# Hybrid block on one core: narrow products between the norm's halves, z tiles in the decay chain, the last output product in two parts, squares added on GpSimd

## The reference

```python
# part 1: 32 heads of 64, state 128 (one B, C per head)
proj = LN(x) @ Win.T                      # x_ssm, z, B, C, dt
xc, Bc, Cc = silu(causal_conv4(...))      # each
h = exp(dt*A) * h + (dt*xc) outer Bc;  y = h . Cc
y = y * rsqrt(mean(y*y) + 1e-6) * silu(z);  x += y @ Wout.T
# part 2 and 4: 16 routed experts, the best 2 by sigmoid, and 2 shared
y = gelu(x @ g) * (x @ w1 + b1) @ w2 ;  x += sum_e weight_e * y_e   (x: normalized)
# part 3: 64 heads of 8, state 128, one B, C for all
x_, B, C = silu(causal_conv4(...)); dt = softplus(.)
state as above; y = y + D*x_
y = y * rsqrt(mean(y*y over 512) + 1e-5) * norm_w * silu(z);  x += y @ out_proj
```

## Time and profile before

| what | us |
|---|---|
| median of 3 runs | 1175.32 (1175.06 to 1180.73) |
| the profiled execution | 1177.91 |
| its span, first to last instruction | 1176.6 |
| PE busy | 1059.7 (90%) |
| VectorE busy | 806.9 (69%) |
| GpSimd busy | 645.0 (55%) |
| ScalarE busy | 576.2 (49%) |

### The profile page before, as it was taken

The page is one execution under the profiler, slowest core; times in us unless marked ns, Lnnn a source line. Parts: engine busy times, 40 slices in busy tenths (PEclk is TensorE's granted clock), DMA queues, the critical chain, the costliest instruction groups (busy, mean ns, idle before and its releaser), DMA issues.

```text
span 1176.6 us, 23865 instructions
## 1 busy us (share of the span) xinstructions
PE 1059.7 (90%) x9928; PEld 875.5 (74%) x9928; DVE 806.9 (69%) x1229; ACT 576.2 (49%) x887; POOL 645.0 (55%) x633
## 2 busy tenths in 40 slices
PE   5489999999999999999967999996688997799998
PEld 3378788888888888888855888884464576588887
DVE  5687888898888889888756346556557864645554
ACT  3677777666777766677413122224463440322221
POOL 3345667776666777666542567552346532265562
PEclk9899999999999999999987999997699977799999
DMA  3302111121112112110200533201121101043221
GB/s 102 103 28 73 64 72 38 64 73 46 58 61 72 45 56 73 46 43 22 64 3 28 187 126 118 89 1 63 40 80 26 31 13 55 33 148 126 94 82 36
DMA packets 47217, 75.96 MB, mean 65 GB/s; under 512 B 11330, under 2 KB 34150, under 8 KB 47110
## 3 DMA queue, kind: packets, MB, share of 16 engines
q1 hardware_dynamic: 47110, 74.44, 19.3%
HBM read 68.13 MB, written 2.36 MB: 60 GB/s over the span
## 4 chain that ended last, share of the span: by engine, by line
PE 65%; DVE 20%; ACT 7%; POOL 4%; issue 3%; DMA 1%; SPq 1%; DVEq 0%; POOLq 0%; ACTq 0%
PE psum L618 33%; PE psum L809 8%; DVE arena L1453 5%; PE psum L685 5%; PE psum L727 4%; PE psum L595 4%; DVE arena L1490 3%; PE psum L677 2%; PE psum L629 1%; ACT arena L1054 1%; PE psum L979 1%; DVE v L1741 1%; POOL arena L1908 1%; PE psum L908 1%; PE psum L873 1%
## 5 line engine op out<-in xcount | busy, mean ns | idle before, releaser
L618 PE MATMUL psum<-vT,split 128*128 128x512 f32 x2136 | 544.9, 406 | 24.8 <-DVE arena L1706 11.9
L618 PEld LDWEIGHTS psum<-vT,split 128*128 128x128 f32 x2136 | 400.0, 193 | 113.3 <-DVE arena L1706 14.7
L1453 DVE SCALAR_TENSOR_TENSOR arena<-psum,arena 128x1023 f32<-128x1023 f32 (+2 forms) x208 | 265.5, 1277 | 83.6 <-ACT arena L1054 64.5
L1881 POOL TENSOR_TENSOR split<-arena,split 128x256 fp32r<-128x256 f32 x178 | 133.4, 759 | 118.4 <-ACT split L1006 118.2
L1054 ACT ACTIVATE arena<-psum,arena 128x512 f32<-128x512 f32 x160 | 108.0, 689 | 143.6 <-PE psum L618 143.2
L2003 POOL TENSOR_TENSOR arena<-arena,bcast 128x512 f32<-128x512 f32 x64 | 83.1, 1299 | 110.5 <-ACT arena L1178 110.5
L1603 DVE SCALAR_TENSOR_TENSOR arena<-psum,arena 128x512 f32<-128x512 f32 x72 | 53.9, 749 | 129.2 <-POOL arena L2003 121.7
L1178 ACT ACTIVATE arena<-psum,arena 128x512 f32<-128x512 f32 x72 | 49.5, 688 | 182.7 <-PE psum L618 182.7
L809 PEld LDWEIGHTS psum<-split_down,split_hid 128*128 128x128 f32 x864 | 114.3, 192 | 7.8 <-DVE split_hid L1614 1.1
L1908 POOL TENSOR_TENSOR arena<-arena,v 128x1021 f32<-128x1021 f32 x32 | 76.7, 2397 | 74.2 <-DVE arena L1453 74.2
L809 PE MATMUL psum<-split_down,split_hid 128*128 128x256 f32 x864 | 116.6, 285 | 0.7 <-DVE split_hid L1614 0.7
(11 more groups left out here) (180 smaller groups left out, 1476.5 us busy)
## 6 DMA issues: line engine op xcount, KB each, us to landing
bcast<-scratch_a SPq DMA_DIRECT2D x32, 512.0 KB, 3.8
bcast<-scratch_e SPq DMA_DIRECT2D x32, 512.0 KB, 4.0
arena<-in_w_a SPq DMA_DIRECT2D x16, 768.0 KB, 4.4
arena<-in_wg SPq DMA_DIRECT2D x36, 128.0 KB, 3.5
arena<-in_wu SPq DMA_DIRECT2D x36, 128.0 KB, 3.4
arena<-in_wd SPq DMA_DIRECT2D x36, 128.0 KB, 3.7
arena<-in_wout_a SPq DMA_DIRECT2D x8, 256.0 KB, 4.4
vT<-arena SPq DMA_DIRECT2D x2, 1024.0 KB, 6.0
```

The source lines that it names most:

```text
L618: m = pe.matmul(bank, split[:, t % SPLITS, i, q, :], vT[:, j, q, half * BANK:(half + 1) * BANK], start=(n == 0), stop=(n == 3 * KD - 1))
L1453: dve.scalar_tensor_tensor(out=tile[:, s:T], in0=bank[:, 0:T - s], scalar=cw_a[:, j, i, TAPS - 1 - s:TAPS - s], in1=tile[:, s:T], op0=ALU. ...
L1881: pool.tensor_tensor(split[:, t % SPLITS, 1], raw, split[:, t % SPLITS, 0].bitcast(F32), ALU.subtract).then_inc(sem["split"], 1)
```

## The change

- **Norm.** `low(0)`, `low(1)`, `low(2)` move to steps 7, 8 and 10, so that statistics and scaling of the later chunks no longer stand behind them, and the narrow weights are split at step 6. In the first head the narrow weights are split there too.
- **Narrow product between the halves.** On TensorE `head` makes: two norm banks, the first half of the narrow product, `between`, two norm banks, the second half, the transpose. `between` is nothing in the first layer, the first half step of the experts (`up(0)`), or half of tile c0 in the second layer. In the first layer tile 0's product comes after all of it.
- **Loads.** SP issues the first weight pair ahead of three small loads. The second experts' weights are loaded once the last state product is done (they lie on Ct, Bs and the piece buffer now), and the router's weights earlier.
- **z tiles.** The second layer's order is c0, c1, z0, z1, z2, decay sums, c2, c3, scores, c4, c5, z3, with the wide buffers by the list `WIDE_B`. The memset of the pad comes after the last GpSimd add.
- **Last output in two parts.** `last_out(0)` makes the products of the second last pair's part before the last transposes, `last_out(1)` adds the last pair's, both in banks 0 to 3. In the second layer the output products of tiles 0 to 2 come before the last sums, those of tile 3 after them.
- **Squares.** The squares of tile 0 go to a buffer of their own, those of tiles 1 and 2 are added to it by GpSimd after quads 11 and 14, and TensorE sums twice (that buffer, then tile 3's squares) into the same eight columns. VectorE divides and adds epsilon in one step, and GpSimd takes the power.
- **Expert weights.** The first two experts' splits move ahead of the norm on ScalarE and GpSimd.

```diff
+SEQ_B = [("c", 0), ("c", 1), ("z", 0), ("z", 1), ("z", 2), ("c", 2), ("c", 3), ("c", 4), ("c", 5), ("z", 3)]
+WIDE_B = [0, 1, 0, 0, 0, 0, 1, 0, 1, 0]
+LOW_AT = {NC - 1: 0, NC: 1, NC + 2: 2}
...
@@ tensor_program
+            def head(width, k, units, n, between):
+                layer_norm(k, 0)
+                layer_norm(k, 1)
+                narrow_half(width, k, units, n, 0)
+                between()
+                layer_norm(k, 2)
+                layer_norm(k, 3)
+                narrow_half(width, k, units, n, 1)
...
+                def last_out(i):
+                    g = PAIRS // GROUP - 1
+                    on.wait_ge(sem["dve_done"], N_DVE["F", PAIRS - 2 + i, 1])
+                    for c in range(NC):
+                        m = pe.matmul(psum[:, c * D:(c + 1) * D], gated_a[:, g % 2, i, c * P:(c + 1) * P],
+                                      wout_a[:, g % 2, i, :], start=(i == 0 and c % 2 == 0), stop=(i == 1),
+                                      skip_group_check=True)
...
+                head(HA, 0, [("dt0", "a"), ("dt1", "a"), ("dtT", "a")], 0, lambda: None)
                 project(0, 0)
-                narrow_product(HA, 0, [("dt0", "a"), ("dt1", "a"), ("dtT", "a")], 0)
...
+                last_out(0)
                 give_back(PAIRS - 1)
-                project_out([("O", PAIRS // GROUP - 1, q) for q in range(4)])
+                last_out(1)
...
-                narrow_product(E, k, narrow_units(n), 2 * n + 1)
-                up(0)
+                head(E, k, narrow_units(n), 2 * n + 1, lambda: up(0))
...
+                head(HB, 2, [("dt0", "b"), ("dt1", "b"), ("dtT", "b")], 2, lambda: project(0, (0,)))
+                project(0, (1,))
+                for n in range(1, 5):
+                    project(n)
...
-                sum_squares(XT - 1)
+                for c2 in range(0, NC, 2):
+                    open_bank(("out", c2))
+                    project_out(c2, range(XT - 1))
+                on.wait_ge(sem["y_out"], 2 * XT - 2)
+                on.wait_ge(sem["sq_acc"], len(ADD_AT))
+                sum_squares(squares, True)
+                on.wait_ge(sem["squared"], XT)
+                sum_squares(B["Bt"], False).then_inc(sem["sq"], 1)
+                on.wait_ge(sem["gates"], XT)
+                for c2 in range(0, NC, 2):
+                    project_out(c2, (XT - 1,)).then_inc(sem["unit"], 1)
...
@@ scalar_program, second layer
-                weights(6)
-                first_tap(2)
-                weights(7)
-                first_tap(3)
-                weights(8)
+                for i in range(3):
+                    gate(i)
+                    weights(6 + i)
...
+                for p in range(2):
+                    expert_weights(1, p)
                 square(XT - 1)
...
@@ vector_program
-                    if late == NC and between:
+                    if late == NC - 2 and between:
                         between()
...
-                        if c % 2 == 0 and c:
-                            low(c // 2 - 1)
+                    if late in LOW_AT:
+                        low(LOW_AT[late])
...
+                on.wait_ge(sem["sq"], 1)
+                dve.tensor_scalar(B["rms"], wide[0][:, 0:NC], 1.0 / WB, 1e-5, ALU.mult, ALU.add).then_inc(sem["rms"], 1)
...
@@ gpsimd_program
+                    if k in ADD_AT:
+                        on.wait_ge(sem["squared"], ADD_AT.index(k) + 2)
+                        pool.tensor_tensor(squares, squares, B["Bt"], ALU.add).then_inc(sem["sq_acc"], 1)
+                for p in range(2):
+                    expert_weights(1, p)
                 on.wait_ge(sem["rms"], 1)
-                pool.tensor_scalar(B["rms"], B["rms"], 1e-5, None, ALU.add).then_inc(sem["rms"], 1)
```

More of the change, by code:

```diff
@@ L101, in norm_behind @@
             order.append(last[late // 2])
-        c = late - LATE
-        if c > 0 and c % 2 == 0:
-            order.append(("ln", k, c // 2 - 1))
+        if late in LOW_AT:
+            order.append(("ln", k, LOW_AT[late]))
     return order + [("ln", k, NC // 2 - 1)]
-def last_outs_in_a():
-    return [("O", PAIRS // GROUP - 1, q) for q in range(4)]
 def decay_units(side):
@@ L128, in filled_in_a @@
     last = PAIRS - 1
[L129 to L130 removed]
+    return order + out_unit(PAIRS, 0) + out_unit(PAIRS, 1) + [("F", last, 0), ("F", last, 1)]
 def emptied_by_dve_in_a():
@@ L298 @@
  gelu gated hid hid_hi hid_lo down down_hi down_lo ones_e router res x_out exp_step
- bconst cw_half fixed pad piece masked masked_p heads ud_b st_half tile_y y_out squared gates rms x_b""".split()
+ bconst cw_half fixed pad piece masked masked_p heads ud_b st_half tile_y y_out squared gates rms x_b x_a x_s sq_acc sq""".split()
 def hybrid_block(nc, io):
@@ L402, in hybrid_block, with wide_b @@
         row_buf = bcast
+        def wide_b(kind, i):
+            return wide[WIDE_B[SEQ_B.index((kind, i))]]
         def expo_buf(k, j):
@@ L923, in finish, with sum_squares, project_out @@
                     m.then_inc(sem["tile_y"], 1)
[L925 to L927 removed]
+                def sum_squares(src, first):
                     for c in range(NC):
[L929 to L934 removed]
+                        m = pe.matmul(wide[0][:, c:c + 1], chunk(src, c), ones[:, 0:1], start=(first and c == 0),
+                                      stop=not first, skip_group_check=True)
+                    return m
+                def project_out(c2, tiles):
+                    bank = bank_of(("out", c2))
+                    for c in (c2, c2 + 1):
+                        for i in tiles:
+                            m = pe.matmul(bank[:, (c % 2) * D:(c % 2 + 1) * D], zc_b[:, i, c * P:(c + 1) * P],
+                                          wout_b[:, i, :], start=(i == 0 and c == c2), stop=(i == XT - 1),
+                                          skip_group_check=True)
+                    return m
+                head(HB, 2, [("dt0", "b"), ("dt1", "b"), ("dtT", "b")], 2, lambda: project(0, (0,)))
+                project(0, (1,))
+                for n in range(1, 5):
+                    project(n)
                 on.wait_ge(sem["decay"], n_decay("b", "lo"))
@@ L2114, in gpsimd_program @@
             first_layer()
+            for p in range(2):
+                expert_weights(0, p)
             experts(0)
```

309 lines of the change are left out of this document (143 added, 166 removed).

## The result

The changed kernel takes 1157.94 us (median of 4 runs, 1156.69 to 1163.82), the one before 1176.38 on the same chip: ratio 0.984, 95% interval 0.980 to 0.988, 18.4 us off. A second set of six runs gave 0.983 (0.981 to 0.986). The forecast was 1157.0.

The account below looks back on a forecast made before the run. The prediction took relays of small steps at four stage heads, not throughput, as the bound. Its terms 2.5 + 4 + 10 + 1.8 = 18.3 us took the median from 1175.32 to 1157.0 us, range 1149 to 1168.

Parts of the forecast that it names:

- The signs named beforehand: Decay sums about 826 us; TensorE waits at most 4 us before last output product; no ones-products in loop; VectorE gapless after rms.
- D: Expert loops: TensorE at the lower clock makes steps slower; level at 5 steps, 7 of 72 give about 1186 us; chance 0.03.
- Head 1: First layer's start: narrow halves ahead of the wide product, row bank about 5 us sooner, partly given back; 2.5 us off.
- Head 2: Before the first experts: 16 output records fill idle time, narrow product and norm reordered; 4 us off, bounds 1 and 6.5.
- Head 3: Second layer: three z tiles ahead of the decay sums, largest term; 10 us off, bounds 5 and 13.
- Rival A: Second layer: serial terms, taps and GpSimd adds bind the last product; head 3 gives only 3 us, 1164 us; chance 0.18.
- The additional table load: Second layer, ScalarE: silu between logarithm and exponential costs one more activation table, about 2.7 us by the skill's rule.
- Tail and head 4: Second layer's end to second routing: 5 us saved in the quad loop leave 1.8 us, bounds -1 and 5.
- I take 5 us: Quad loop: three groups of ones-products, 6.7 us, leave it; 5 us taken because VectorE's masks end some waits; bounds 3 and 6.7.
- B: All heads: clock stays at the lower level; heads 1, 2, 4, 3 give 0.5, 1, -1.5, 7; 1168 us; chance 0.07.
- E: Whole kernel: nothing moves the end, each step waiting for a transfer; 1175 us; chance 0.03.
- C: All four terms at their warm bounds, 4.5 + 6.5 + 13 + 5 less a little overlap; 1148 us; chance 0.07.

Follow-up runs that it names:

- e6: Changed kernel with the first layer's last output product whole, 32 records behind the last normalization instead of 16 before and 16 behind: 1165.97 us, ratio 0.988.
- e5: Changed kernel with the first expert half behind the whole head, not between its narrow halves, before both expert stages: 1157.49 us, ratio 0.982.
- e8: Changed kernel with two light convolution tiles (1 and 3) in the second layer instead of four: 1157.32 us, ratio 0.981.
- e1: Changed kernel once more, nothing edited, for a second profile: 1160.96 us, ratio 0.983.
- e4: Changed kernel with the second experts' first weight loads, casts and subtractions as late as before: 1161.23 us, ratio 0.984.
- e10: Changed kernel with GpSimd's two adds of squares left out, the 32 ones-products kept: 1159.47 us, ratio 0.981.
- e3: Changed kernel with the first three tiles' ones-products back in the quad loop and GpSimd's two adds of squares gone: 1165.93 us, ratio 0.988.

## Why the prediction was right, and where its terms were off

The median lies 0.9 us from the forecast. That is closer than either is known: the 18.4 us have an interval of 4.6 either way, and the terms below are off by 0.6 to 2.3 us each, in both directions, so part of the agreement is luck. By the stages, 16.9 us come off in the mean of two profiles each where the forecast had 18.3; no single profile would have shown it, since two of one kernel differ by 9 us.

The signs named beforehand came: the decay sums at 824.5 us for 826, TensorE's wait for the last normalization at 1.26 us for 4.71, no ones-products in the quad loop, VectorE without an idle gap from 973.48 us to the end of the second low part. Masks above 1 us, a sign of being wrong in most quads, were 6 and 3 of 40 for 4 and 4 before. The sums have small slips: 623.5 and 1.9 are 625.4, not 625.6; 0.23 us is the time of one record, not of 16; D's 7 steps give 1185, not 1186. None changes the forecast.

**Head 1.** 2.5 us forecast, 3.5 measured. The two profiles of the kernel before differ by 2.3 here, so the 1 us means nothing. The gain itself is seen in all eleven profiles of the new head, 31.2 to 33.0 us for 34.7 and 37.0, but no run took its parts alone.

**Head 2.** The steps came as forecast, shifted by the 1.8 us of head 1: first add 602.4 less 1.8 is 600.6, seen at 600.41; second low part 611.5, seen to end at 611.08; the narrow half 2.6, seen 2.72; the expert half 3.9, seen 3.25; the exponential 623.8, seen 622.92. e6 shows that the split of the output product carries the whole gain, since without it the stage is that of the kernel before; so the other edits of this head come to nothing together there, and none of them was run alone but the expert half. This half, which I counted with 3.9 us inside the new order and never as an edit of its own, is worth nothing in head 2 and costs 1 to 4 us in head 4 (e5).

**Head 3.** The three products took 4.61, 3.02 and 3.02 us for 4.6, 3.5 and 3.0, the silus 1.02. The decay sums stand at 824.5 for a forecast of 826, the last projection ends at 854.0 where 861.6 less 6.5 is 855.1. The 2.3 us up to the softplus sum were too many: 0.9. Rival A was not beside the forecast but inside it. The sum already ran along the chain of terms, taps and adds, with GpSimd's 2.4 us twice, and e8 shows that this chain is the bound: half of it gone, 4.2 us gained at once. A rival that names the same mechanism as a term of the sum should have been written as its size. The additional table load cost nothing: it runs at 813.30 us for 1.28 us, and ScalarE then still waits 1.86 for the product. The Trainium skill, ScalarE: Activation LUTs, section Rules for kernel authors, would have priced the switch at about 2.7 us; this trace disagrees with both the size and the effect. The load ahead of this one starts at 811.36 us, right behind the term, and the activation behind it at 812.66, so a switch takes 1.30 us in all.

**Tail and head 4.** The step that was mis-sized is "I take 5 us" for the ones-products that leave the quad loop: 2.7 in two profiles each, 3.0 over the nine. I had expected masks to refill the time. It was mostly the issue gaps, which the rows of the kernel before did show (0.3 us beside L929 in the earlier trace rows) but which I treated as constant. The contention was foreseen in kind: the Trainium skill, GPSIMD Engine Reference, section Key points, says that VectorE and GpSimd contend for SBUF when VectorE reads two inputs there. The trace agrees with one mask of 2.82 us; that it would be the last mask, with TensorE behind it, I had not seen. Of the two or three masks that I allowed for, one was stretched beyond 1.8 us, in one profile of nine. Then the 12.1 us of output product were 10.6 and 12.4, two groups of ones-products 3.6 for 4.4, the power 1.7 and the norm from the first add to the second low part 11.4 for 11.7. The forecast for the way from finish to routing was 3.2 us longer than before; it is 1.9.

**The others.** B fell: the second and third z products of head 3 ran in 3.02 us each (granted clock 1.00), and the last 16 output records of the first layer in 3.72, though the first narrow half of head 2 did run at the lower level (2.72). D fell: from 640 to 780 us the mean clock is 0.98, for 0.96 between 645 and 785 us before, and the stage of the second experts is longer by 0.8 us only. E fell with the result. C needed every bound at its warm end.

## What to carry to other kernels

Where TensorE waits for a late small result, look for work of its own that is already due and split a product to fit the gap: the 16 records in an idle 4.7 us gave the whole gain of head 2, and the reordering of halves beside them gave none. Work put ahead of a critical small step must be shorter than the time until its input is ready: 48 records in front of the ones-products cost 5 us that 12 did not. When busy time is taken out of a loop that already has gaps, expect part of it back (here half), and take two profiles of each kernel before believing a stage.

## What the runs showed of the hardware

The quad loop of one and the same program took 101.6 us in one execution and 97.0 in another, at granted clocks of 0.90 and 0.95. Behind a wait of 4.71 us and eight transposes, the last 32 output records of the first layer ran at a mean granted clock of 0.72 (e6, 9.90 us); behind one of 1.26 us, the last 16 ran at 1.00 (3.72 us). There the longer wait went with a slower product as well; no run changed the wait alone. Behind the mask wait of 3.56 us not even that can be said, since the finish takes the same 3.67 us in profiles without such a wait.

In all ten profiles without ones-products in the loop, the first 98 of the 128 small records of one quad (the eleventh) are followed by 2.2 to 2.7 us in which TensorE waits for nothing that the profile shows, each time at the same record (e1):

```profile
923.44 1.18 PE L941 MATMUL psum<-bcast,arena 64*32 64x64 f32 x98 [1.08 <-issue]
...
926.79 0.45 PE L941 MATMUL psum<-bcast,arena 64*32 64x64 f32 x30 [2.16 <-issue]
```

Neither the loads (e4) nor the adds (e10) move it. With ones-products in the loop (the kernel before twice, e3) it isn't there; the longest gap is then one of 1.2 to 2.0 us in the last quad, 2 to 4 records before its end. So the place goes with the program. The page of the changed kernel's first profile lists transfers of another kind besides the kernel's own:

```profile
q8 instruction: 78, 1.28, 0.4%
```

These are 78 packets of 16 KB. In all thirteen profiles the longest issue gap of the quad loop ends 1.2 to 1.6 us after one of them has landed: 929.09 us behind 927.58, and 926.79 behind 925.38 in e1. Of the 67 such gaps over 0.6 us, 48 end like that. One packet comes every 5.5 us or so, so chance would give less than a tenth. This points to TensorE's own instructions arriving late, but no run here changed their loading: it is argued, not shown.
